# Macaron block with a Mamba-like scan on 8 cores: two changes of layout done by transposing DMAs instead of TensorE, and the scan's output kept by token

## What is computed

```python
# x: (16, 4096, 1024) float32
x = x + 0.5 * _L0_ffn_ref(_layernorm(x, axis=-1), L0_ffn_weight)     # sign(weight) as matrix
x = x + _L0_attn_ref(_layernorm(x, axis=-1), ...)
x = x + 0.5 * _L0_ffn_ref(_layernorm(x, axis=-1), L0_ffn_weight)

def _L0_attn_ref(...):                       # 8 heads of 256 channels, state 64
    x = input_tensor @ Wx.T                  # 1024 -> 2048
    z = input_tensor @ Wz.T
    x = jax.nn.silu(_causal_conv(x, conv_w, conv_b))
    b, c = x @ Wb.T, x @ Wc.T                # 8 heads x 64 each
    dt = jax.nn.softplus(x @ Wdt.T + b_dt)
    # per token: state = exp(dt * a) * state + (dt * b) x^T ;  y = c . state
    y = _ssd_scan(xh, b, c, dt, a)
    y = y + d_param[None, None, :, None] * xh
    # mean and variance of y per sequence and head, over all tokens
    yn = (yg - mean) / jnp.sqrt(var + EPS) * gn_w + gn_b
    return (yn * jax.nn.silu(z)) @ Wout.T
```

## Time and profile before

| What | Value |
|---|---|
| Median of 2 runs | 8058.15 us (8045.68 to 8070.62) |
| The profiled execution's own time | 8038.02 us |
| Span of its slowest core (core 4) | 8036.2 us |
| Spans of the 8 cores | 8001.9 to 8036.2 us |
| Busy: TensorE, DVE, ACT, POOL | 53%, 42%, 23%, 3% |
| Moved by DMA | 309.23 MB, mean 38 GB/s |

### The profile page before, as it was taken

How to read it: one execution, slowest core, us unless ns; L and a number is a source line. 1 busy time by engine, 2 the same in 40 slices (tenths; PEclk the granted TensorE clock), 3 DMA queues, 4 the chain that set the end, 5 groups by cost and what they waited for, 6 DMA issues and landing times.

```text
span 8036.2 us, 73752 instructions; the slowest of 8 cores (8001.9 to 8036.2 us)
## 1 busy us (share of the span) xinstructions
PE 4292.1 (53%) x18851; PEld 2018.1 (25%) x18851; DVE 3340.5 (42%) x9115; ACT 1818.9 (23%) x4200; POOL 245.3 (3%) x349
## 2 busy tenths in 40 slices
PE   2254455463555555556666656666665354454554
PEld 0121122121222222233333333333332121221222
DVE  2244444453444444443434443444433444444444
ACT  0022222222222222111111111111111222222222
POOL 0000000000000000000000000000000000000000
PEclk9977777786777777766666666666665676676776
DMA  2201111111111111200000110000101221221221
GB/s 32 33 27 40 35 32 33 33 36 30 32 32 33 36 36 33 50 26 30 22 22 22 32 32 22 22 22 22 43 22 27 76 68 63 71 68 61 74 68 45
DMA packets 208924, 309.23 MB, mean 38 GB/s; under 512 B 12641, under 2 KB 143978, under 8 KB 208514
## 3 DMA queue, kind: packets, MB, share of 16 engines
q0 software_dynamic: 45472, 136.37, 6.8%
q1 hardware_dynamic: 163042, 168.14, 6.4%
HBM read 189.15 MB, written 150.99 MB: 42 GB/s over the span
## 4 chain that ended last, share of the span: by engine, by line
PE 39%; DVE 20%; issue 16%; ACT 13%; DMA 9%; DVEq 1%; SPq 1%; ACTq 0%; POOL 0%; POOLq 0%
PE pt L422 5%; PE pb L553 4%; PE pb L502 4%; PE pb L454 4%; PE pb L719 3%; PE pb L814 3%; PE pt L774 3%; ACT G L409 3%; PE pb L736 3%; ACT dumpA L362 3%; DVE acc_a L1035 3%; DVE G L883 3%; PE pb L1094 2%; DVE G L429 2%; PE pt L336 2%
## 5 line engine op out<-in xcount | busy, mean ns | idle before, releaser
L422 PE MATMUL pt<-identc,G 128*128 128x128 bf16 x1536 | 391.5, 266 | 1697.0 <-ACT G L409 1496.4
L553 PE MATMUL pb<-G,slotB 128*128 128x512 bf16 x2048 | 516.5, 398 | 428.3 <-ACT xpB L511 243.8
L429 DVE COPY G<-pt 128x128 bf16<-128x128 bf16 x1536 | 345.2, 225 | 779.1 <-PE pt L422 635.9
L422 PEld LDWEIGHTS pt<-identc,G 128*128 128x128 bf16 x1536 | 156.3, 105 | 1955.7 <-issue 1954.9
L825 ACT ACTIVATE G<-pb,colT 128x128 bf16<-128x128 f32 x512 | 188.1, 367 | 1548.5 <-PE pb L814 1511.2
L502 PE MATMUL pb<-G,slotA 128*128 128x512 bf16 x2048 | 517.0, 398 | 0.0
L362 ACT ACTIVATE dumpA<-G 128x512 bf16<-128x512 bf16 x384 | 241.3, 628 | 1214.9 <-DVE G L464 622.0
L1070 PE MATMUL pb<-slotB,G 128*128 128x512 bf16 x2048 | 449.8, 381 | 35.4 <-DVE G L1046 35.4
L1042 ACT ACTIVATE acc_b<-G 128x256 f32<-128x256 bf16 x512 | 209.8, 415 | 1016.7 <-DVE G L1046 962.0
L553 PEld LDWEIGHTS pb<-G,slotB 128*128 128x128 bf16 x2048 | 188.1, 100 | 753.8 <-issue 585.6
L883 DVE TENSOR_SCALAR_CACHE_REDUCE G<-pb 128x256 bf16<-128x256 f32 x512 | 217.5, 425 | 320.1 <-ACT dumpA L893 196.4
(11 more groups left out here) (159 smaller groups left out, 6717.6 us busy)
## 6 DMA issues: line engine op xcount, KB each, us to landing
sp_xc<-G SPq DMA_DIRECT2D x64, 512.0 KB, 3.0
sp_z<-G POOLq DMA_DIRECT2D x64, 512.0 KB, 3.7
G<-sp_xc SPq DMA_DIRECT2D x64, 512.0 KB, 7.0
sp_y<-G POOLq DMA_DIRECT2D x64, 512.0 KB, 5.2
G<-sp_y SPq DMA_DIRECT2D x128, 256.0 KB, 4.2
G<-sp_z POOLq DMA_DIRECT2D x128, 256.0 KB, 3.7
out<-G SPq DMA_DIRECT2D x64, 512.0 KB, 3.2
G<-x POOLq DMA_DIRECT2D x32, 512.0 KB, 9.0
```

Source lines behind the costliest of these rows:

```text
L422: emit=lambda e, tt=tt, kt=kt, bank=bank: e.transpose(bank[:, kt * 128:(kt + 1) * 128], src[:, tt * D + kt * 128:tt * D + (kt + 1) * 128], ...
L429: e.tensor_copy(out=dst[:, kt * chunk + tt * 128:kt * chunk + (tt + 1) * 128], in_=bank[:, kt * 128:(kt + 1) * 128]))
L553: last = e.matmul(bank[:], slotB[:, k * INNER + ot * 128:k * INNER + (ot + 1) * 128], u2_rhs(k, pp), start=(k == 0), stop=(k == KD - 1))
```

## The change

Three things change together.

1. In the scan, the 16 transposes and 4 copies of each sub-chunk go. In their place SP issues one transposing DMA of 512 KB per sub-chunk, which reads `sp_xc` in DRAM (2048 rows of 128 tokens) and writes `xtm` (L770 after).
2. `ymm` swaps its operands: the mask `v_mg` and the C matrix are the weights, `xtm` and `S_bf` are streamed, 256 columns at a time. y then has tokens on partitions, `yt` is token-major, and so is `sp_y`. The store is one DMA of 2 MB per chunk instead of four of 512 KB.
3. In stage 3 y is needed by channel. Each of the four y loads of 256 KB is replaced by four transposing DMAs of 64 KB: 16 in a chunk, each reading 256 rows of 128 channels of `sp_y` (L1003 after). z is loaded as before.

```diff
-    sp_y = nc.dram_tensor("sp_y", [BPC, INNER, L], BF16, kind="Internal").ap()
+    sp_y = nc.dram_tensor("sp_y", [BPC * L, INNER], BF16, kind="Internal").ap()
...
-                    for grp in range(4):
-                        bi = grp % 2
-                        bank, bkey = ptr[bi], PT[bi]
-                        for qq in range(4):
-                            q = grp * 4 + qq
-                            p.op("pe", ["xcs", "ident"], [bkey],
-                                 emit=lambda e, q=q, qq=qq, bank=bank, t0=t0:
-                                 e.transpose(
...
-                        p.op("dve", [bkey], [xkey],
...
+                    xv = bass.AP(sp_xc.tensor, b * INNER * L + T0 + t0,
+                                 [[L, INNER], [1, 128]])
+                    p.op("sp", ["sp_xc"], [xkey],
+                         emit=lambda e, xv=xv, xtm=xtm: e.dma_start(
+                             out=xtm[:], in_=xv, transpose=True), dma=True)
...
                                 e.matmul(sl,
-                                         xtm[:, ct * 128:(ct + 1) * 128],
                                          v_mg[:, h * 128:(h + 1) * 128],
+                                         xtm[:, h * 256:(h + 1) * 256],
                                          start=True, stop=False)
...
-                                    S_bf[:, (h // 2) * HD + (ct % 2) * 128:
-                                         (h // 2) * HD + (ct % 2) * 128 + 128],
                                     cpad[:, (h // 2) * CH_B + t0:(h // 2) * CH_B + t0 + 128],
+                                    S_bf[:, (h // 2) * HD:(h // 2) * HD + HD],
...
-                for q in range(4):
-                    y_view = bass.AP(sp_y.tensor, b * INNER * L + q * 4 * 128 * L + T0,
-                                     [[L, 128], [128 * L, 4], [1, CH_B]])
...
+                y_view = bass.AP(sp_y.tensor, (b * L + T0) * INNER,
+                                 [[INNER, 128], [128 * INNER, NSUB], [1, INNER]])
+                dma("pool", y_view,
+                    bass.AP(v_yt.tensor, 0, [[8192, 128], [2048, NSUB], [1, 2048]]),
+                    ["yt"], ["sp_y"])
...
+            for ot in range(KI):
+                y_view = bass.AP(sp_y.tensor, (b * L + T0) * INNER + ot * 128,
+                                 [[INNER, CH_A], [1, 128]])
+                p.op("sp", ["sp_y"], [kyr],
+                     emit=lambda e, y_view=y_view, v_yr=v_yr, par=par, ot=ot:
+                     e.dma_start(
+                         out=bass.AP(v_yr.tensor, par * 4096 + ot * CH_A,
+                                     [[8192, 128], [1, CH_A]]),
+                         in_=y_view, transpose=True), dma=True)
             for q in range(4):
-                y_view = bass.AP(sp_y.tensor, b * INNER * L + q * 4 * 128 * L + T0,
-                                 [[L, 128], [128 * L, 4], [1, CH_A]])
-                dma("sp",
...
```

More of the change, by code:

```diff
@@ L766, in build_program @@
                     btkey = "btmA" if su % 2 == 0 else "btmB"
-                    for grp in range(4):
-                        bi = grp % 2
-                        bank, bkey = ptr[bi], PT[bi]
-                        for qq in range(4):
-                            q = grp * 4 + qq
-                            p.op("pe", ["xcs", "ident"], [bkey],
-                                 emit=lambda e, q=q, qq=qq, bank=bank, t0=t0:
-                                 e.transpose(
-                                     bank[:, qq * 128:(qq + 1) * 128],
-                                     v_xcs[:, q * CH_B + t0:q * CH_B + t0 + 128],
-                                     ident[:]))
-                        p.op("dve", [bkey], [xkey],
[L779 to L782, removed]
+                    xv = bass.AP(sp_xc.tensor, b * INNER * L + T0 + t0,
[3 more added lines that the diff above has]
+                             out=xtm[:], in_=xv, transpose=True), dma=True)
                     for h in range(8):
@@ L860, in ymm @@
                             last = None
-                            for q in range(4):
-                                ct = 4 * j + q
-                                h = ct // 2
-                                sl = psum[j][:, q * 128:(q + 1) * 128]
+                            for hh in range(2):
+                                h = 2 * j + hh
+                                sl = psum[j][:, hh * 256:(hh + 1) * 256]
                                 e.matmul(sl,
-                                         xtm[:, ct * 128:(ct + 1) * 128],
                                          v_mg[:, h * 128:(h + 1) * 128],
+                                         xtm[:, h * 256:(h + 1) * 256],
                                          start=True, stop=False)
@@ L878, in build_program @@
                              emit=ymm)
-                        for half in range(2):
-                            col = c * NSUB * 8 + su * 8 + j * 2 + half
+                        for hh in range(2):
+                            h = 2 * j + hh
+                            col = c * NSUB * 8 + su * 8 + h
                             p.op("dve", [ykey], ["ys", "yt"],
-                                 emit=lambda e, j=j, su=su, half=half, col=col:
+                                 emit=lambda e, j=j, su=su, hh=hh, h=h, col=col:
                                  e.tensor_scalar(
[L884 to L887, removed]
+                                     out=v_yt[:, su * 2048 + h * 256:
+                                              su * 2048 + (h + 1) * 256],
+                                     in0=psum[j][:, hh * 256:(hh + 1) * 256],
                                      scalar1=1.0, scalar2=0.0, op0=ALU.mult,
@@ L891, in build_program @@
                             p.op("act", [ykey], ["yss", "dumpA"],
-                                 emit=lambda e, j=j, half=half, col=col:
+                                 emit=lambda e, j=j, hh=hh, col=col:
                                  e.activation(
                                      out=dumpA[:, 0:256],
-                                     in_=psum[j][:, half * 256:(half + 1) * 256],
+                                     in_=psum[j][:, hh * 256:(hh + 1) * 256],
                                      func=AF.Square, accum_out=yss[:, col:col + 1]))
@@ L1012, in p2_loads @@
             kyr, kzr = f"yr_{par}", f"zr_{par}"
-            for q in range(4):
-                y_view = bass.AP(sp_y.tensor, b * INNER * L + q * 4 * 128 * L + T0,
-                                 [[L, 128], [128 * L, 4], [1, CH_A]])
-                dma("sp",
-                    bass.AP(v_yr.tensor, par * 4096 + q * 4 * CH_A,
-                            [[8192, 128], [CH_A, 4], [1, CH_A]]),
-                    y_view, ["sp_y"], [kyr])
+            for ot in range(KI):
[7 more added lines that the diff above has]
+                         in_=y_view, transpose=True), dma=True)
+            for q in range(4):
                 z_view = bass.AP(sp_z.tensor, b * INNER * L + q * 4 * 128 * L + T0,
```

## The result

The changed kernel takes 8256.52 us in the median of 11 runs (8216.15 to 8329.88), the one before 8053.24 us (10 runs). The ratio is 1.0243, with an interval of 1.0205 to 1.028: slower by 2.4%. In the longest execution, 8329.88 us, the cores of one die were granted a lower clock than the others, and the ratio leaves it out. The forecast was 8334 us and slower; its range of 7870 to 9150 holds the time.

What follows compares the result with a forecast made beforehand. Engine-to-engine chains bound the kernel, with the y load's latency bare in stage 3. Losses of 546 and 15 us less 285 gained make +276 on 8038: 8314, or 8334 us as median, range 7870 to 9150.

Steps and rivals of the forecast that it cites:

- What bounds it: Scan and stage 3: a chain from engine to engine sets the pace; stage 3's y load latency is bare.
- Part 1: Scan: without the transposes and copies of x, DVE's work on B starts earlier; 285 us gained.
- Part 2: Scan, ymm: 16 matmuls of 256 columns for 32 of 128, and the single y store, change nothing; zero.
- Part 3: Scan: the double-buffered transposing loads of x stay hidden unless one takes more than 24 us; zero.
- Part 4: Stage 3: 16 unhidden transposing y loads a chunk, each costing t = 1.3 us; 546 us lost over 30 chunks.
- The count of row pieces: Stage 3: 4096 row pieces a chunk at 50 ns on 16 engines give t = 0.8, or 1.6 with turning.
- geometric middle: Stage 3: t = 1.3 as the middle between 0.36 and 4.87 us, the shortest and longest y request issue.
- rival C: Stage 3: blocks of a transposing request go one after another, 2.6 us each; +945 us, 8983 us; chance 0.15.
- rival A: Stage 3: a transposing request costs what a plain one does, 0.65 us; -53 us, 8005 us; chance 0.30.
- 16 t + 4.84: Stage 3: bare time of a chunk's y load, 16 requests of t plus 4.84 us behind the last issue.
- The sum: Whole kernel: 546 + 15 - 285 = +276 us on the profiled execution's 8038, giving 8314, or 8334 as median.
- A sign that did not come: Scan and stage 3: the granted clock was to stay near 0.63 and 0.69.

Runs made afterwards that it cites:

- x alone: Kernel before with only the TensorE transposes and copies of x replaced by one transposing DMA per sub-chunk: 7778.71 us, ratio 0.9671.
- the run with eight: Kernel before with each sub-chunk's x loaded by 16 transposing requests of 32 KB, eight DMA waits standing behind DVE's: 7875.02 us, ratio 0.9785.

## Why the prediction was right, point by point

- **What bounds it.** Right. The y load's latency was bare and each us added to it came back in the turn: 467 us more waiting, 471 us more stage 3. Moved out of the way it costs nothing in a turn, in either kernel.
- **Part 1, 285 us.** Right in kind, a little too large. Alone it gave 261 to 265 us in the scan of core 0 and of core 3. With the order of waits put right in both kernels it is 272 (2809.9 less 2538.2): 7 us of the shortfall are the wait on x's DMA behind DVE's in `ymm`, which the forecast did not have. The last 13 us I can't place.
- **Part 2, nothing.** Right: 6 us, with the single store of y counted in. Half as many weight loads bought nothing.
- **Part 3, hidden.** Right. No matmul waited for x, and even sixteen requests a sub-chunk stayed hidden.
- **Part 4, t = 1.3.** The value came out at 1.28 us (20.5 us for 16 in most turns), but not for the reason weighed. The count of row pieces had nothing to do with it: a request of 32 KB costs the same as one of 128 KB. My geometric middle was luck as to its size. The Trainium skill's VectorE: DVE Perf Modes, section The three transpose paths, gives 1309 ns for one block of 128 by 128; a request with one such block took 1.28 us here and one with four 1.31, so it is not a price per block, and rival C falls. The Trainium skill's Advanced Engine Details and Errata, section X-Bar Transpose (TRN2), holds that a transposing DMA is as fast as a regular one; for the issue the trace disagrees, 1.28 us against 0.65, and by that rule rival A would have come true.
- **The term that was mis-sized** is the tail behind the last request, "16 t + 4.84". I took 4.84 from four requests of 256 KB and left it as it was for sixteen small ones. Behind those it is 1.83 us in the turn shown (7044.40 to 7046.23). Over all turns of core 4 its median falls from 4.4 to 1.6 us. A 64 KB request lands 2.4 us after its issue and they follow each other every 1.28 us, so the earlier ones have landed while SP still issues the last. 2.8 us too much in 30 turns is 84 of the 561 us that I had put down as lost. Two smaller ones are 8 us for t = 1.3 instead of 1.28, and 4 us at the opening, which cost 11 us more than before and not 15 (first data after 21.7 us instead of 17.7, the second chunk 21.1 us behind it instead of 13.7). That leaves 465 of the 471 us measured.
- **The sum.** +276 us forecast on the profiled execution, +228 measured (and +203 between the medians): 90 too much lost in stage 3, some 60 too much gained in the scan on core 4 (223 of 285, about 40 of it the clock, below), and 20 us less in stage 1, where nothing was changed. That the misses partly cancel is luck.
- **A sign that did not come.** I expected the granted clock of stage 3 to stay near 0.69. On core 4 it fell from 0.70 to 0.64 over the stage, and the matmuls with Wout went from 381 to 405 ns. It cost next to nothing: on core 0 they took 380 ns in both kernels, and its stage 3 is as long (2249.6 us against 2249.8).

## What to carry to other kernels

Before a load is made slower, look at what stands in its shadow: the same 16 requests made stage 3 478 us longer or 20, by their place in SP's list alone. From 32 to 128 KB a transposing DMA was priced by the request and not by the byte, and at 512 KB not much higher, so make them as large as the layout allows: one of 512 KB hid easily where sixteen left SP 4 us in 24. And write the wait that ends last as the last one, since those behind it are worked off only then.

## What the runs showed of the hardware that I had not expected

- A transposing request holds SP's queue for about 1.2 us at 32, 64 and 128 KB (medians 1.18, 1.19 and 1.21) and for 1.85 us at 512 KB. A plain one of 256 KB held it for 0.50. Whether that is SP's own work, or whether what takes the requests holds SP back, no run separates.
- A transposing request of 512 KB lands 8.4 us after its issue in the changed kernel (median), a plain one of 512 KB from the same tensor 6.2; with x alone it is 12.5 against 5.9. Why it takes longer there was not looked for; the cover hid both.
- Waits on semaphores that are long fulfilled still cost 0.11 us each when they stand behind a late one (median gap 0.15 us with none, 0.26 with one, 1.03 with eight). In the run with eight, the table of waits put that time down to a DMA in 45 of 64 sub-chunks.
- The granted clock fell in pairs of cores and in single stretches, in stages that the change doesn't touch. In the changed kernel's profiled execution stage 1 was granted 0.75, 0.75, 0.78, 0.79, 0.76, 0.76, 0.74 and 0.74 on cores 0 to 7; before it was 0.78 or 0.79 on all. On core 4 it was also lower in the scan, 0.62 against 0.64 on core 3 (3500 to 6000 us). Matmuls of the projections there:

```profile
L719 PE MATMUL pb<-G,slotA 128*128 128x512 bf16 x1024 | 279.5, 445 | 0.0
...
L736 PE MATMUL pb<-G,slotA 128*128 128x512 bf16 x1024 | 250.7, 402 | 0.0
```

Before they took 422 and 380 ns, 259.9 and 232.0 us in all, so up to 38 of the 47 us that core 4's scan gained less than core 3's are this; on core 3 of the same execution they were as before (257.4 and 232.0 us), and its scan gained 270 us. Why the clock falls so was not tried.
